# Four graph layers fused on one core: another order of the steps in the repeating turn

## What is computed

```python
h = jnp.maximum(_layernorm(x, axis=-1), 0.0)
x = x + L0(h, adj)   # incidence H = (adj != 0): two hypergraph convolutions, a layer norm between them
h = jnp.maximum(_layernorm(x, axis=-1), 0.0)
x = x + L1(h, adj)   # transition = rows of adj * exp(leaky_relu(sj + si)), normalized; relu(h W0 + T h W1 + T T h W2 + b)
h = jnp.maximum(_layernorm(x, axis=-1), 0.0)
x = x + L2(h, adj)   # 8 heads: relu(tanh(adj * (Xc Xp^T)) Xp)
h = jnp.maximum(_layernorm(x, axis=-1), 0.0)
x = x + L3(h, adj)   # relu((adj h) K), rows without input masked
```

## Time and profile before

| | |
|---|---|
| median of 3 runs | 1710.2 us (1709.0 to 1710.37) |
| the profiled execution | 1713.86 us |
| its span | 1712.0 us |
| PE busy | 1512.7 us (88%) |
| DVE busy | 1158.8 us (68%) |
| ACT busy | 907.6 us (53%) |
| POOL busy | 295.5 us (17%) |
| DMA | 92.07 MB, queue 1 16.0% of 16 engines' span |

### The profile page before, as it was taken

The page is one execution under the profiler, slowest core; times in us unless marked ns, Lnnn a source line. Parts: engine busy times, 40 slices in busy tenths (PEclk is TensorE's granted clock), DMA queues, the critical chain, the costliest instruction groups (busy, mean ns, idle before and its releaser), DMA issues.

```text
span 1712.0 us, 26942 instructions
## 1 busy us (share of the span) xinstructions
PE 1512.7 (88%) x9850; PEld 1099.2 (64%) x9850; DVE 1158.8 (68%) x2528; ACT 907.6 (53%) x1511; POOL 295.5 (17%) x343
## 2 busy tenths in 40 slices
...
DMA packets 58543, 92.07 MB, mean 54 GB/s; under 512 B 4288, under 2 KB 23296, under 8 KB 58496
## 3 DMA queue, kind: packets, MB, share of 16 engines
q1 hardware_dynamic: 58496, 91.44, 16.0%
...
## 4 chain that ended last, share of the span: by engine, by line
PE 56%; issue 21%; DVE 12%; ACT 6%; POOL 2%; DMA 1%; SPq 0%; ACTq 0%; POOLq 0%; DVEq 0%
PE ring_f L1013 35%; PE ring_b L1272 7%; PE ring_b L1013 7%; PE pv_acc L1288 4%; DVE bns L760 3%; DVE att L959 2%; PE ring_f L1181 2%; POOL rstd L434 2%; ACT hf L482 1%; DVE rows L860 1%; DMA x_in<-in_x 1%; DVE rows L910 1%; DVE xc_s L784 1%; ACT xp_n L472 1%; PE ring_f L1149 1%
## 5 line engine op out<-in xcount | busy, mean ns | idle before, releaser
L959 DVE TENSOR_TENSOR att<-ring_b,at 128x1024 f32<-128x1024 f32 x256 | 306.0, 1219 | 104.2 <-PE ring_b L1272 103.7
L611 ACT ACTIVATE att<-att 128x1024 f32<-128x1024 f32 x256 | 262.6, 1053 | 145.3 <-DVE att L959 143.4
L434 POOL TENSOR_TENSOR rstd<-var,mhalf 128x4 f32<-128x4 f32 x80 | 81.0, 1012 | 865.1 <-DVE var L775 865.1
L1013 PE MATMUL ring_f<-w,uz 128*128 128x256 f32 (+1 forms) x896 | 192.3, 337 | 5.1 <-DVE w L676 4.6
L1013 PE MATMUL ring_f<-m,tr_h 128*128 128x256 f32 x1024 | 190.7, 287 | 0.0
L1272 PE MATMUL ring_b<-xc_t,xp_t 32*128 32x512 f32 x1024 | 158.3, 690 | 33.3 <-DVE att L959 32.2
L1013 PEld LDWEIGHTS ring_f<-m,tr_h 128*128 128x128 f32 x1024 | 158.8, 191 | 34.1 <-issue 34.1
L1013 PEld LDWEIGHTS ring_f<-w,uz 128*128 128x128 f32 x896 | 153.0, 193 | 43.0 <-issue 11.7
L1288 PE MATMUL pv_acc<-att,xp_n 128*32 128x512 f32 x1024 | 140.2, 620 | 19.1 <-ACT att L611 19.1
L1013 PEld LDWEIGHTS ring_f<-m,inc_n 128*128 128x128 f32 x1024 | 127.7, 194 | 44.1 <-issue 30.6
L1013 PE MATMUL ring_f<-m,inc_n 128*128 128x256 f32 x1024 | 135.3, 289 | 20.3 <-POOL m L438 18.9
...
## 6 DMA issues: line engine op xcount, KB each, us to landing
at<-in_adjT SPq DMA_DIRECT2D x32, 1024.0 KB, 6.7
rows<-in_adjT SPq DMA_DIRECT2D x16, 1024.0 KB, 5.3
adj_n<-in_adj SPq DMA_DIRECT2D x16, 1024.0 KB, 5.3
...
```

The source lines that it names most:

```text
L434: pool.tensor_tensor(rstd[k][:], var[k][:], mhalf[:], ALU.pow).then_inc(rstd_made[k].sem, 1)
L611: act.activation(v, v, ACT.Tanh).then_inc(tanh_made.sem, 1)
L959: dve.tensor_tensor(att[:, u % 2, 2 * half:2 * half + 2], ring_b[half][:], at[:, u % NT].unsqueeze(1).broadcast_to([P, 2, N]), ALU.mult).t ...
L1013: ins = pe.matmul(dst, lhsT, rhs, start=(first and n == 0), stop=(last and n == len(pairs) - 1), skip_group_check=True)
```

## The change

Only the five tables of steps are changed: no step is added or removed, none is changed inside, and the rotation of the banks stays. Two tables also start their turn at another step (ACT's turn now begins behind `f_tt` 2, DVE's behind unit 6 half 1), so the same step has another delay there; the order along the stream is what counts. PE's table in full, of the others the lines that are spoken of:

```diff
 PE
-                    (0, f_m, 0), (2, k_attend, 2), (0, f_m, 1), (2, k_scores, 4), (0, f_u, 0), (0, f_u, 1),
+                    (0, f_m, 0), (0, f_m, 1), (2, k_attend, 2), (2, k_scores, 4), (0, f_u, 0), (0, f_u, 1),
...
-                    (0, f_zT, 0), (0, f_zT, 1), (0, f_zT, 2), (0, f_zT, 3), (0, f_xw, 0), (0, f_xw, 1),
-                    (2, k_attend, 6), (0, f_xw, 2), (0, f_xw, 3), (2, k_outT, 0), (2, k_attend, 7), (0, f_m2, 0),
-                    (0, f_m2, 1), (1, k_hT), (2, k_outT, 1), (0, f_y, 0), (0, f_y, 1), (1, k_xp, 0), (1, k_xp, 1),
+                    (0, f_zT, 0), (0, f_zT, 1), (1, k_hT), (0, f_zT, 2), (0, f_zT, 3), (0, f_xw, 0), (0, f_xw, 1),
+                    (0, f_xw, 2), (0, f_xw, 3), (2, k_attend, 6), (0, f_m2, 0), (0, f_m2, 1), (2, k_outT, 0),
+                    (2, k_attend, 7), (0, f_y, 0), (2, k_outT, 1), (0, f_y, 1), (1, k_xp, 0), (1, k_xp, 1),
...
-                    (0, f_q, 0), (0, f_q, 1), (0, f_q, 2), (2, k_ax, 0, 0), (0, f_q, 3), (2, k_ax, 0, 1),
-                    (2, k_ax, 1, 0), (2, k_ax, 1, 1), (2, k_out, 0), (0, f_tt, 0), (0, f_tt, 1), (2, k_out, 1),
-                    (0, f_tt, 2), (0, f_tt, 3), (0, f_r1), (1, k_scores, 0), (0, f_r, 0), (1, k_scores, 1),
-                    (0, f_r, 1), (1, k_attend, 0), (1, k_scores, 2), (0, f_x1), (1, k_attend, 1), (1, k_scores, 3),
+                    (0, f_q, 0), (0, f_q, 1), (2, k_ax, 0, 0), (0, f_q, 2), (0, f_q, 3), (2, k_ax, 0, 1),
+                    (2, k_ax, 1, 0), (2, k_ax, 1, 1), (2, k_out, 0), (2, k_out, 1), (0, f_tt, 0), (0, f_tt, 1),
+                    (0, f_tt, 2), (1, k_scores, 0), (0, f_tt, 3), (0, f_r1), (1, k_scores, 1), (0, f_r, 0),
+                    (1, k_attend, 0), (0, f_r, 1), (1, k_scores, 2), (0, f_x1), (1, k_attend, 1), (1, k_scores, 3),
...
 SP
-                    (1, next_adjt), (2, next_at), (0, next_wrow), (3, next_at2), (4, store), (0, next_x),
+                    (1, next_adjt), (0, next_x), (2, next_at), (0, next_wrow), (4, store), (2, next_at2),
                     (0, next_adj),
 POOL
-                    (0, p_rstd, 0), (3, k_y, 0), (3, k_y, 1), (0, f_h0, 0), (0, f_h0, 1), (3, k_y, 2), (3, k_y, 3),
+                    (0, p_rstd, 0), (0, f_h0, 0), (3, k_y, 0), (0, f_h0, 1), (3, k_y, 1), (0, f_h0, 2),
 DVE (hops)
-                    (2, k_unit, 1, 0), (2, k_unit, 1, 1), (1, f_r, 0), (2, k_unit, 2, 0), (0, f_h0),
+                    (2, k_unit, 1, 1), (1, f_r, 0), (0, f_h0), (2, k_unit, 2, 0), (1, f_r, 1), (0, f_dn, 1),
```

More of the change, by code:

```diff
@@ L650, in turn @@
-                    (0, f_relu, 1), (2, k_unit, 4, 1), (0, f_relu, 2), (0, f_relu, 3), (2, k_unit, 5, 0),
-                    (2, k_unit, 5, 1), (0, f_z, 0), (0, f_z, 1), (0, f_z, 2), (0, f_z, 3), (0, f_zT, 0),
-                    (0, f_zT, 1), (0, f_zT, 2), (1, k_h2, 0), (1, k_h2, 1), (0, f_zT, 3), (1, k_h2, 2),
-                    (2, k_unit, 6, 0), (2, k_unit, 6, 1), (2, k_unit, 7, 0), (2, k_unit, 7, 1), (0, f_xw, 0),
-                    (0, f_xw, 1), (1, k_h2, 3), (2, k_xh, 1), (0, f_m2, 0), (0, f_m2, 1), (1, k_hT), (1, k_xp, 0),
@@ L655, in turn @@
-                    (1, k_xp, 1), (0, f_h1, 0), (0, f_h1, 1), (0, f_h1, 2), (0, f_h1, 3), (2, k_h3, 0),
-                    (0, f_hT, 0), (0, f_hT, 1), (2, k_h3, 1), (2, k_h3, 2), (1, k_xc), (0, f_q, 0), (2, k_h3, 3),
-                    (0, f_q, 1), (0, f_exp, 0), (0, f_q, 2), (0, f_exp, 1), (0, f_q, 3), (0, f_exp, 2),
-                    (0, f_exp, 3), (1, k_xn), (2, k_ax, 0),
+                    (0, f_h0, 0), (0, f_h0, 1), (0, f_h0, 2), (2, k_unit, 0, 0), (1, f_tt, 3), (2, k_unit, 0, 1),
@@ new lines, in turn @@
+                    (0, f_z, 1), (0, f_z, 2), (0, f_z, 3), (0, f_zT, 0), (0, f_zT, 1), (0, f_zT, 2),
+                    (2, k_unit, 6, 0), (0, f_zT, 3), (2, k_unit, 6, 1), (2, k_unit, 7, 0), (0, f_xw, 0),
+                    (2, k_unit, 7, 1), (0, f_xw, 1), (1, k_hT), (0, f_m2, 0), (0, f_m2, 1), (2, k_xh, 1),
+                    (1, k_xp, 0), (1, k_xp, 1), (0, f_h1, 0), (0, f_h1, 1), (0, f_h1, 2), (0, f_h1, 3),
+                    (2, k_h3, 0), (0, f_hT, 0), (0, f_hT, 1), (2, k_h3, 1), (2, k_h3, 2), (2, k_h3, 3), (1, k_xc),
@@ L659, in turn @@
+                    (0, f_q, 0), (0, f_exp, 0), (0, f_q, 1), (0, f_q, 2), (0, f_exp, 1), (0, f_q, 3),
+                    (0, f_exp, 2), (2, k_ax, 0), (1, k_xn), (0, f_exp, 3), (2, k_ax, 1), (2, k_out, 0),
+                    (2, k_out, 1), (0, f_tt, 0), (0, f_tt, 1), (0, f_tt, 2),
                 ))
@@ L987, in turn @@
-                    (1, f_q, 3), (1, f_mask, 1), (1, f_max, 2), (1, f_mask, 2), (1, f_max, 3), (3, k_mask),
-                    (3, k_ax, 0), (1, f_mask, 3), (1, f_sums), (3, k_ax, 1), (1, f_trans, 0), (1, f_trans, 1),
-                    (1, f_trans, 2), (1, f_trans, 3), (1, f_tt, 0), (1, f_tt, 1), (1, f_tt, 2), (2, k_unit, 0, 0),
-                    (2, k_unit, 0, 1), (1, f_tt, 3), (0, f_HT, 0), (0, f_dn, 0), (0, f_HT, 1), (0, f_HT, 2),
-                    (2, k_unit, 1, 0), (2, k_unit, 1, 1), (1, f_r, 0), (2, k_unit, 2, 0), (0, f_h0),
```

46 lines of the change are left out of this document (25 added, 21 removed).

## The result

The changed kernel takes 1671.9 us (median of 4 runs, 1669.7 to 1673.0) against 1709.6 us of the kernel before on the same chip: ratio 0.978, 95% interval 0.976 to 0.980.

A forecast was written before the change was run, and what follows sets the result against it. PE's list was taken as the path, its work plus its waits. 0.5 + 0.8 - 0.2 + 0.47 - 0.1 = 1.47 us a turn, times 14, plus 2.0 and 0.5, made 23.1 us: 1687 us, range 1676 to 1705.

The forecast's parts named there:

- Up to k_scores 7: PE's stretch to k_scores 7: its wait vanishes, k_attend 5 waits about 2.2 us; gain 0.5 us a turn.
- k_hT among the z transposes: k_hT moved into the z transposes falls into their bank wait: gain 0.8 us a turn.
- f_m2's cover: Behind f_m2, the place k_hT leaves: k_outT and a k_attend now cover the same wait for m2.
- Unit 7 half 1: On DVE between the second and third low part of f_zT, delaying the second f_xw: loss 0.2 us a turn.
- First k_ax piece: Between second and third f_q on PE, it covers the 0.47 us bank wait: gain 0.47 us a turn.
- The hops: k_scores 0 and k_attend 0 earlier, DVE tight, f_dn slower beside POOL: loss 0.1 us a turn, bounds 0 and 0.7.
- x: The load of x goes out 17 us earlier, into slack; no gain was counted.
- five waits of a turn: PE's waits: 0.79 and 1.38 us at units 5 and 7, 0.23 before f_xw, 0.47 at f_q, 1.41 at k_out.
- The ends: Outside the full turns: 2.0 us from k_xp's wait in turn 16, and 0.5 us in turn 1.
- the rival with 0.15: Clock stays up around the z transposes: 12 turns gain another 0.78 us, 9.4 us, giving 1678 us; chance 0.15.
- The slower rival: The 2.2 us gap before k_scores 7 drops the clock at once: 3.0 us a turn, 1729 us; chance 0.10.

The follow-up runs named there:

- a_bn: The changed kernel with three of the second norm's statistics again behind the last f_conv1 on DVE, not two: 1680.1 us.
- a_hT2: The changed kernel with k_hT on PE back behind k_attend 7, and ACT's copy of k_hT behind f_m2 and k_xh 1: 1684.6 us.
- b_hT: The kernel before with the change of b_h2, and PE's k_hT between the second and third group of z transposes: 1727.8 us.
- a_hT: The changed kernel with k_hT on PE back behind k_attend 7, ACT untouched: 1748.4 us.
- b_q: The kernel before with only PE's first piece of k_ax moved ahead of the third f_q: 1726.9 us.
- b_x: The kernel before with only the load of x moved ahead of the burst of loads: 1700.6 us.
- b_h2: The kernel before with ACT's four k_h2 among and behind the relus, ahead of tanh 5, and DVE's offset 3 moved: 1715.7 us.
- a_q: The changed kernel with PE's first piece of k_ax back behind the third f_q: 1676.4 us.
- a_kax: The changed kernel with ACT's first copy of k_ax back behind the last exp and xp_n: 1676.8 us.

## Why the prediction was wrong, point by point

**What bounds the kernel: right.** PE's list is the path, and in the full turns of these kernels nearly all that was gained or lost is a PE wait or PE's clock.

**Up to k_scores 7: right.** Forecast 0.5 us, measured 0.43 from the stretch and 0.40 from a_bn. The wait at k_scores 7 is gone as said. k_attend 5 waits 1.53, not 2.2 us, since another 0.72 us stand ahead of k_attend 4 (k_xh 0 behind the third relu on ACT), a wait that the forecast did not see; the idle time between k_attend 4 and k_scores 7, 2.25 us, is what it said.

**k_hT among the z transposes: right.** Forecast 0.8, measured 0.79 from the stretch and 0.85 from a_hT2. b_hT and a_hT show that this holds only in company, which the text on f_m2's cover had half said.

**Unit 7 half 1: too dear by 0.2 us.** The second f_xw waits for nothing. The third low part comes as late as laid out: the forecast had it end 6.0 us behind the start of k_scores 7, and it does so at 823.8, 5.9 us behind. But PE is not as early. With k_hT in the block the first f_xw still starts 4.32 us behind k_scores 7 and the second 6.24 us behind (824.15), where the forecast had 5.9, so the low part is there first.

**First k_ax piece: right in size, 0.47 against 0.52 and 0.55 us, with one premise wrong.** The inputs of k_ax are not "a turn old": ACT writes the last h in the same turn, and in b_q the piece waited 0.34 us for it. The new ACT list, with all of k_h3 earlier, is what makes the term true. The sentence that the 1.41 us ahead of k_out "moves along and stays" is true of after; b_q shows that without the new orders of ACT and DVE the wait grows to 2.08 us, and a clock loss of about 1.4 us came with it in 10 turns.

**The hops: 0.16 lost against 0.1 forecast**, within the bounds, but not by the cause that was named. PE waits for nothing in the hops of after, as before, and DVE's four f_dn of a turn take 3.07 us together, against 3.62 before: beside POOL 0.95 and 0.75 instead of 1.23 and 1.02 us, and 0.69 us alone in both. What makes the 0.16 us is open. The rule of the Trainium skill, page "SBUF — State Buffer", section "Who interferes with whom", by which the loss could have reached 0.7 us, was not borne out in that size; that f_dn is slower beside POOL agrees with it.

**x: the step that failed among the waits.** The forecast said x is "loaded 17 us earlier, into slack", and put it at nothing. Before the change there was no slack: x came 0.47 to 0.99 us late for DVE in turns 3 to 14, f_hT waited for it, and this was 0.48 us in turn 8 and 0.4 us a turn in the mean, 6 to 7 us. The two rows shown above stand in the trace of before. The forecast named five waits of a turn; this one of 0.52 us was left in the remainder and not followed to its releaser. b_x shows the cause by itself. (17 us is what b_x moves the load by; in after it goes out 25 us earlier in the turn.)

So the waits came to 2.07 instead of 1.47 us a turn: 29 instead of 20.6 us in 14 turns. With the forecast's ends, 2.5 us, that alone would have been 1678 us against the median, still inside the range.

**The ends: 3.8 instead of 2.5 us, and not where they were put.** The wait of k_xp in turn 16 fell from 2.02 to 0.78 us, but PE waits elsewhere instead, and the way from k_out of turn 15 to that of turn 16 takes 70.03 instead of 70.49 us: 0.5, not 2.0 us. Turn 17 gave 2.6 us (58.04 to 55.47), which the forecast had not; no run says why.

**The clock: the rival with 0.15 that happened.** What spoke against it was only that the wait "is now one gap", and it is two, 0.72 and 1.53 us. The runs show how little such an argument carries: in b_h2 more idle time than before, in fewer pieces, went with one low turn. The price was low too: 0.78 us was read from turn 8, whose block took 5.10 us, but in eight of the twelve low turns it took 5.29 or 5.30, 0.97 us over the 4.32, and the turns say 0.9 (98.2 against 99.1, and 96.5 against 97.4 in a_bn). It gave 11.3 us in the profiled pair. Waits and clock together, 40 us, and the ends are the 44.1 us of the spans. Against the medians, 37.7 us, some 5 us are left for the clock (an estimate: 37.7 - 29.0 - 3.8); the profiled execution of before, at a mean clock of 0.960, was one of its low ones. The missed wait and the clock were both needed to leave the range, and why the clock stays up in after is not shown.

**The slower rival: a true mechanism, wrong in size.** A gap of 1.53 us behind one of 0.72 never dropped the clock in the z block, in five profiled executions (after, a_hT, a_hT2, a_q, a_kax). One of 2.71 us did in 10 of 14 turns, for 1.0 to 1.5 us each, not the 3.0 us a turn that it was given.

**Range and chances.** The range was built from one failure at a time. It had no case in which a missed wait and the clock went the same way, and its lower end, 1676 us, was little more than the clock rival alone (1678).
